# Gated experts of the third lane: two scalar copies in one, and the product made by GpSimd alone

## The reference, cut to what matters

```
shared = (silu(x @ gate_w) * (x @ up_w)) @ down_w           # 256 hidden features: two units of 128
for e in range(8):
    g, u = x @ fc1_w[e][:, :128], x @ fc1_w[e][:, 128:]
    y   += combine[:, e] * ((silu(g) * u) @ fc2_w[e])       # combine: top 2 of 8, renormalised
x = x + tanh(g_ffn[1]) * (shared + y)
```

## Time and profile before

| | |
|---|---|
| time, median of 3 runs | 2339.2 us |
| span of the profiled execution | 2336.6 us |
| its own time | not given apart; the median lies 2.6 us over the span |
| busy share of the span: PE, DVE, ACT, POOL | 88%, 84%, 63%, 41% |
| mean granted TensorE clock | 0.953 of full speed |
| the six blocks with the changed code | 825.1 us of the span, 136.8 to 139.2 us each |
| L1706, the operation that VectorE loses | 60 times, 25.2 us busy |

### The profile page before, as it was taken

How to read it: one execution, slowest core, us unless ns; L and a number is a source line. 1 busy time by engine, 2 the same in 40 slices (tenths; PEclk the granted TensorE clock), 3 DMA queues, 4 the chain that set the end, 5 groups by cost and what they waited for, 6 DMA issues and landing times. The chain is left out here.

```text
span 2336.6 us, 41635 instructions
## 1 busy us (share of the span) xinstructions
PE 2065.4 (88%) x12569; PEld 1613.8 (69%) x12569; DVE 1956.1 (84%) x7828; ACT 1479.0 (63%) x3637; POOL 948.2 (41%) x1374
## 2 busy tenths in 40 slices
PE   5878798989999899998999899898999999888677
PEld 3556577657976578766886579675887669767466
DVE  1299797989989898998989899897989979797882
ACT  3546467776767666776566667676667766477341
POOL 3233213544254434544255443544245541443441
PEclk9989999999999999999999999999999999899798
DMA  4000101000100101001100001001010001101000
GB/s 185 1 8 1 35 23 33 1 5 31 55 4 1 35 6 53 1 1 35 42 17 1 22 14 55 4 1 35 6 53 1 1 28 51 35 1 55 1 3 3
DMA packets 29503, 55.03 MB, mean 24 GB/s; under 512 B 2914, under 2 KB 10082, under 8 KB 28642
## 3 DMA queue, kind: packets, MB, share of 16 engines
q1 hardware_dynamic: 29282, 52.37, 6.8%
HBM read 51.31 MB, written 1.05 MB: 22 GB/s over the span
## 5 line engine op out<-in xcount | busy, mean ns | idle before, releaser
L232 DVE MATCH_REPLACE8 top_work<-top_eight,top_work 128x256 f32<-128x256 f32 x1664 | 684.2, 429 | 0.0
L234 DVE MAX8 top_eight<-top_work 128x8 f32<-128x256 f32 x1664 | 633.6, 432 | 0.2
L268 POOL TENSOR_TENSOR top_p<-top_p,top_rest 128x512 f32<-128x512 f32 x192 | 244.6, 1274 | 221.3 <-ACT top_rest L261 221.2
L789 PE MATMUL bank<-workP 128*128 128x256 f32 x1024 | 276.9, 395 | 9.1 <-POOL workP L949 4.0
L927 ACT ACTIVATE att_pP<-bank,att_tinyP 128x256 f32<-128x256 f32 x512 | 215.5, 477 | 67.6 <-DVE att_tinyP L976 66.5
L789 PEld LDWEIGHTS bank<-workP 128*128 128x128 f32 x1024 | 180.3, 193 | 56.2 <-issue 32.8
L976 DVE TENSOR_REDUCE att_tinyP<-bank 128x2 f32<-128x512 f32 x256 | 174.7, 689 | 22.8 <-PE bank L789 21.7
L234 DVE MAX8 top_lead<-bank 128x8 f32<-128x256 f32 x384 | 149.0, 440 | 43.2 <-PE bank L594 18.0
L261 ACT ACTIVATE top_rest<-top_work,top_nmax 128x256 f32<-128x256 f32 x384 | 173.9, 505 | 10.6 <-DVE top_work L232 10.0
L949 POOL TENSOR_SCALAR workP<-workP,const 128x256 f32<-128x256 f32 x256 | 122.3, 483 | 128.6 <-PE bank L789 91.6
L240 POOL TENSOR_SCALAR top_nmax<-top_lead 128x2 f32<-128x2 f32 x192 | 37.3, 194 | 333.7 <-DVE top_lead L234 333.1
(11 more groups left out here) (365 smaller groups left out, 4591.1 us busy)
## 6 DMA issues: line engine op xcount, KB each, us to landing
gelu_w<-in_pack3w SPq DMA_DIRECT2D x72, 256.0 KB, 3.0
top_qk<-in_pack3w SPq DMA_DIRECT2D x72, 256.0 KB, 2.8
pack<-in_pack SPq DMA_DIRECT2D x1, 4352.0 KB, 19.7
pack<-in_pack SPq DMA_DIRECT2D x1, 2266.0 KB, 9.8
pack<-in_pack SPq DMA_DIRECT2D x1, 1028.0 KB, 8.5
mix_wb<-in_ctx SPq DMA_DIRECT2D x1, 1024.0 KB, 4.8
x_in<-in_x SPq DMA_DIRECT2D x8, 128.0 KB, 2.3
ctx_tok<-in_ctx SPq DMA_DIRECT2D x8, 128.0 KB, 2.5
```

Source lines behind the costliest of these rows:

```text
L232: ins = nc.vector.match_replace(self.work[:, u % 2, j, :], eight, src, GONE)
L234: ins = nc.vector.max(eight, src)
L268: self.k.nc.gpsimd.tensor_tensor(v, v, self.rest[:, :, :], ALU.subtract).then_inc(self.p_ready, 1)
L789: mm = self.k.nc.tensor.matmul(self.banks[u % 2][:, j * T:(j + 1) * T], self.q1[:, u % self.RING, j * P:(j + 1) * P], self.kT, start=True, ...
```

## The change

ScalarE takes the tanh first, and then copies both halves of the bank in one instruction of 128x512, times 0.5, into a new buffer `halves` (parts 6 and 7 of the workspace `rest`, which nothing else uses in this stage). GpSimd makes `2 * (th + 1)`, then times the first half, then times the second half into `hT`: three instructions, each of which waits for the one before. VectorE has no part in it. With the factor 2, `2 * (1 + tanh) * 0.5 g * 0.5 u` is what it was. The order of steps is as it was.

```diff
@@ class GatedInOneBank, __init__
-        self.th, self.hT = rest[:, 0, :], rest[:, 1:3, :]
+        self.th, self.hT, self.halves = rest[:, 0, :], rest[:, 1:3, :], rest[:, 6:8, :]
@@ act
             act.wait_ge(self.h_ps, u + 1)
-            nc.scalar.activation(self.hT[:, u % 2, :], self.bank[:, T:2 * T], ACT.Copy, scale=0.5).then_inc(self.half_ready, 1)
             if u >= 1:
                 act.wait_ge(self.hT_ready, u)
             nc.scalar.activation(self.th, self.bank[:, 0:T], ACT.Tanh, scale=0.5).then_inc(self.th_ready, 1)
+            nc.scalar.activation(self.halves, self.bank[:, :].rearrange("p (c t) -> p c t", c=2), ACT.Copy,
+                                 scale=0.5).then_inc(self.half_ready, 1)
@@ pool
+            nc = self.k.nc
+            pool.wait_ge(self.th_ready, u + 1)
+            nc.gpsimd.tensor_scalar(self.th, self.th, 1.0, 2.0, ALU.add, ALU.mult).then_inc(self.u_ready, 1)
             pool.wait_ge(self.half_ready, u + 1)
-            pool.wait_ge(self.u_ready, u + 1)
-            hT = self.hT[:, u % 2, :]
-            self.k.nc.gpsimd.tensor_tensor(hT, hT, self.th, ALU.mult).then_inc(self.hT_ready, 1)
+            pool.wait_ge(self.u_ready, 2 * u + 1)
+            nc.gpsimd.tensor_tensor(self.th, self.th, self.halves[:, 0, :], ALU.mult).then_inc(self.u_ready, 1)
+            pool.wait_ge(self.u_ready, 2 * u + 2)
+            nc.gpsimd.tensor_tensor(self.hT[:, u % 2, :], self.th, self.halves[:, 1, :], ALU.mult).then_inc(self.hT_ready, 1)
@@ dve
-        nc, b = self.k.nc, self.bank
+        nc = self.k.nc
...
-        u = self.at(s, 0, 0)
-        if u >= 0:
-            dve.wait_ge(self.half_ready, u + 1)
-            dve.wait_ge(self.th_ready, u + 1)
-            nc.vector.scalar_tensor_tensor(out=self.th, in0=self.th, scalar=1.0, in1=b[:, 0:T], op0=ALU.add,
-                                           op1=ALU.mult).then_inc(self.u_ready, 1)
```

## The result

The changed kernel takes 2351.66 us (median of 4 runs, 2351.30 to 2356.03) against 2339.89 of the kernel before in the same comparison (4 runs): ratio 1.0053, 95% interval 1.0038 to 1.0067. It is slower by some 12 us; the forecast was slower by 6.6. The profiled execution took 2351.37 us, its span is 2349.6.

A forecast was written before the change was run, and what follows sets the result against it. TensorE, nearly even with VectorE, was taken to set the pace, with later waits on GpSimd. TensorE's +1.8 us at unit 8 became +1.1 per block, +6.6 in six: 2345.8 us; 8-in-10 range 2326 to 2356.

The forecast's parts named there:

- The latency: From a unit's first ScalarE instruction to its product's end: 2.58 us, against 2.06 before in unit 5.
- +1.8 us at unit 8: TensorE's summed delay at the start of unit 8, from units 1, 3, 5, 6, 7 and ScalarE's wide copy.
- the adding up of the delays: Delays of units 3, 5, 6 and 7 were to reach the turns at 770 undiminished.
- Units 5 and 6: Products end later on GpSimd, delaying TensorE by +0.52 and +0.50 us, with keep_top waits of 0.8 to 1.1 us.
- Units 3 and 7: Later products on GpSimd: TensorE newly waits +0.52 us for unit 3's, and unit 7's comes +0.27 us later.
- Unit 1: Product there 0.43 us earlier, with TensorE waiting for it; only -0.2 us was kept in the sum.
- Unit 0: Ends 0.5 us later with TensorE busy elsewhere; costed at nothing, up to 0.5 us if that cover is gone.
- The wide copy: ScalarE's copy takes 0.21 us more per unit, counting in units 0, 2 and 8: 0.2 us per block, range 0 to 0.6.
- VectorE's gain: From losing L1706: at most 7.6 us per block, at least nothing; some 0.3 comes back at the block's end.
- The rule: GpSimd holding the shared SBUF ports blocks two-SBUF-input VectorE operations: 0 in the sum, +0.9 us per block at worst.
- Rival (A): VectorE is the bound after all from head 9 on: 1.5 us won per block, -9 us, 2330; chance 0.28.
- Rival (C): Slower by more: VectorE held up at unit 9 and the router, plus a covered unit: +2.5 per block, 2354; chance 0.12.

The follow-up runs named there:

- before_longer: The kernel before, with one more GpSimd tensor_scalar of 128x256 between VectorE's operation and GpSimd's product in all 60 units; ratio 1.0053.
- no_vector: The kernel before, with VectorE's L1706 replaced by a GpSimd tensor_scalar and factor a left out of the product; 2315.4 us, ratio 0.9877.
- before_behind: The kernel before, with GpSimd's product of units 5 and 6 moved behind the keep_top that TensorE waits for; ratio 1.0006.
- no_copy: The kernel before, without ScalarE's copy of the second half, GpSimd multiplying th by itself instead; ratio 1.0061.

## Why the prediction came out right in sum and wrong in part

- **Direction and size.** Slower by 6.6 was forecast, slower by 11.8 measured (9.2 in the repetition, 7.6 in the six blocks that hold the code). The time lies in the range that should hold it, 0.7 us above the forecast's own.
- **The latency.** 2.58 us forecast, 2.57 measured. One term was smaller (0.41 for 0.48), and the first product starts 0.15 us after GpSimd's first instruction in place of 0.08, as it also needs the wide copy. The forecast had set the copy's end against the first GpSimd instruction; it is the second that waits for it.
- **The sum is near by luck in its terms.** The forecast had +1.8 us at unit 8, 0.4 of it absorbed by VectorE's slack at L895 and 0.3 won back at the block's end: +1.1. Measured were +1.44 at head 15's scores, 0.64 absorbed up to L895 and 0.45 lost behind it: +1.25 by the rounded means, +1.27 by the blocks. The step that the prediction called the likeliest to fail, the adding up of the delays, did fail, and terms that it had put at nothing or too low (unit 0, the wide copy, the block's end) filled the place.
- **Units 5 and 6: +0.52 and +0.50.** Measured +0.29 and -0.03. The waits of the earlier trace rows exist, 0.67 for 0.38, 0.53 for 0.57 and 1.27 for 1.23, but the forecast of 0.8 to 1.1 us after units 5 and 6 was wrong. The two delays lie beside each other, not behind each other. After unit 5 TensorE is 0.50 us late, 0.21 of it already by the copy. Unit 6's first ScalarE instruction starts 11.44 us after head 10's scores all the same, as before (11.45), since in the kernel before it stood behind an exponential (L251) and came 0.56 us after its matmul had ended: that much room it had. So unit 6's `keep_top` delays TensorE to the point to which unit 5 had already delayed it. In before_longer, which keeps VectorE's instruction, it is the same: +0.50, then 0.00.
- **Units 3 and 7: +0.52 and +0.27.** Measured +0.31 and +0.24. The wait for unit 3's product came, at 0.36 us.
- **Unit 1, kept at -0.2.** The wait became 0.45 us shorter as worked out (2.66 to 2.22). The means of step 6 to 7 are 11.82 both times, but only because of the third block before: like against like 0.32 us arrived, so the term was near. What failed is the reason behind it: I priced a wait by its length alone. The next 0.54 us of wait (2.22 to 1.68, in no_vector) brought 2.1 us, 1.5 of them by the clock; I had no such term.
- **Unit 0, costed at nothing with "up to 0.5 if the cover is gone".** The cover was gone: +0.46, with a new wait of 0.21 us for L472, which stood behind the product on GpSimd. The wide copy took 0.42 (forecast 0.2), and not where the prediction put it: at unit 5, where ScalarE was to have room, and at unit 8. Together these fill most of the hole that units 3 to 7 left.
- **VectorE's gain.** It is 0.13 us a block behind head 5 (0.37 in the mean). The 0.66 at head 15 is mostly slack of VectorE that TensorE's delay used up, with the new wait of 1.61 us at L895; the forecast had 0.4 absorbed there and a wait of 1.4. At the block's end, where I had 0.3 of gain, L315 came 0.53 us later.
- **The collision at L315.** The rule that the prediction takes from the Trainium skill's page "SBUF — State Buffer" (section "SBUF: two separate sides") is for a VectorE operation with two SBUF inputs. L315 has one tensor input and was held too. The same sentence of the page names a second case, a VectorE operation in a 2-port mode; whether L315 ran in one, no run here shows.
- **Rival (A)**, VectorE as the bound, -9 us: false for this change and half true of the kernel. The argument against it ("0.23 us is all that VectorE could be earlier" at head 9) holds for the stretch from head 8 to head 10, 15.70 us in every kernel, and I stretched it over the block. With the latency of before, no_vector wins 21 us in the six blocks. The two causes don't add: at 2.56 us VectorE's instruction is worth 6.2 us (before_longer against after; somewhat more, as only the second carries the wide copy), at 2.03 us 21.3 (before against no_vector). Either one alone, the instruction away or the latency kept, leaves TensorE's wait in unit 1 at 2.2 us or more.
- **Rival (C)** made the layer norm at the end late by over 0.5 us its condition, and had a hold-up of VectorE on the path. Both happened: L315 started 0.53 us later and was held. But the hold-up was worth 0.14 us, not 0.9.

What stays open: how much of the 4 us beyond the six blocks belongs to the change. The last three stretches took 322.8 us before and 328.0 after, but also 327.8 in before_behind, whose time equals that of before. Over the fourteen profiles the time beyond the six blocks follows the time spent there at the lower clock: a line through them gives 0.28 us for each us, and none lies more than 1.8 us off it. By that estimate 3.3 of the 5.3 us between the two profiles are clock, and why there was more of the lower level in one of them is not shown. And whether a complete kernel reaches no_vector's time: none of the complete ones beat the kernel before, and no_vector leaves a factor out. A kernel with VectorE's instruction kept and the tanh ahead of the copy wasn't tried. That the wait brings the lower clock is read from what followed what, 67 times of 69 and none of twelve; no run changed the wait in unit 1 and nothing else.

## What to carry to other kernels

Work taken off a nearly full engine pays only if the result isn't later where another engine stands waiting: move the instruction, but keep the latency. Test the two apart, and measure the latency in each variant's own trace, since an instruction in another's shadow costs none. A wait of TensorE has a second price, the clock behind it: here 0.45 us less of a wait brought 0.32, and the next 0.54 brought 2.1. Delays of one engine at two places need not add, if what the second hangs on starts no later. And look at a mean over blocks block by block before reading a cause from it.

## What the hardware showed

- Of 69 waits of TensorE of 2.2 to 3.2 us at one place, 67 were followed by a stretch at 1.2 GHz in which the same turns took 1.22 us for 0.70; twelve waits of 1.41 and 1.68 us were followed by none. 0.54 us of wait (2.22 against 1.68) went with 1.5 us of work, and in no_copy, at waits of 2.48 and 2.49 us, blocks with the stretch were 1.4 us longer over the next two steps than the one without.
- A VectorE tensor_scalar of 128x128 with a single tensor operand in SBUF, L315, went from 0.34 to 1.40 us beside a GpSimd tensor_tensor of 128x512, and back to 0.34 when that one was made to wait for it.
- A kernel with 60 ScalarE instructions fewer (no_copy) was 0.6% slower, at a mean granted clock of 0.940.
- GpSimd on 128x256 f32: tensor_scalar 0.42, tensor_tensor 0.73 us, 0.08 between dependent ones.
